# State-space scan: the steps of two 512-column tiles made one 1024-column step, with the product with C split three to one between GpSimd and VectorE

## What is computed

```python
dA = jnp.einsum('bld,dn->bldn', dt, A)
dB_u = jnp.einsum('bld,bld,bln->bldn', dt, u, B)
...
dA_cum = jnp.exp(jnp.flip(jnp.cumsum(jnp.flip(dA_shift, 1), 1), 1))
xs = jnp.cumsum(dB_u * dA_cum, 1) / (dA_cum + 1e-12)
y = jnp.einsum('bldn,bln->bld', xs, C)
...
return y + u * D
```

## Time and profile before

| | us |
|---|---|
| median of 3 runs (7024.77 to 7026.32) | 7026.24 |
| span of the profiled execution | 7017.1 |
| DVE busy in it | 5767.6 |
| POOL busy | 4206.1 |
| ACT busy | 4186.0 |
| PE busy | 5452.5 |

### The profile page before, as it was taken

One profiled execution on the slowest core, in us unless ns is written; L12 is line 12 of the kernel. 1 busy time (PEld: TensorE's weight loads), 2 busy tenths in 40 slices (PEclk: granted clock), 3 DMA queues, 4 the chain that ended last, 5 costly groups with the idle time before them and its releaser, 6 DMA issues. The chain is left out here.

```text
span 7017.1 us, 79490 instructions
## 1 busy us (share of the span) xinstructions
PE 5452.5 (78%) x14584; PEld 2611.9 (37%) x14584; DVE 5767.6 (82%) x8375; ACT 4186.0 (60%) x6495; POOL 4206.1 (60%) x3210
## 2 busy tenths in 40 slices
PE   5777777777777777878786877777777777899978
PEld 2333333333333333333333333333333333556566
DVE  7999999989999999999999999999999998222223
ACT  4767676666767676767676767676767665211100
POOL 3767777777777776767676767676777775000000
PEclk8988888888888888889898989898988898999989
DMA  2333333333333333333342423333333332322355
GB/s 76 115 99 113 102 111 102 109 103 107 106 104 105 107 103 110 108 99 116 95 121 90 122 91 119 94 115 99 114 100 112 102 109 79 93 87 87 92 187 203
DMA packets 554755, 755.05 MB, mean 108 GB/s; under 512 B 123584, under 2 KB 272064, under 8 KB 552192
## 3 DMA queue, kind: packets, MB, share of 16 engines
q1 hardware_dynamic: 554240, 750.73, 34.7%
HBM read 660.80 MB, written 89.75 MB: 107 GB/s over the span
## 5 line engine op out<-in xcount | busy, mean ns | idle before, releaser
L963 PE MATMUL y_ps<-v_ring,ident 128*128 128x512 f32 x4096 | 2388.9, 689 | 858.9 <-POOL v_ring L513 304.3
L504 POOL TENSOR_TENSOR g_ring<-dtu,b_ring 128x512 f32<-128x512 f32 x2048 | 2726.3, 1350 | 40.1 <-DMA b_ring<-bc_scr 27.5
L808 DVE TENSOR_TENSOR_SCAN s_ring<-e_ps,g_ring 128x512 f32<-128x512 f32 x2048 | 2478.8, 1210 | 80.8 <-POOL g_ring L504 80.8
L513 POOL TENSOR_TENSOR v_ring<-z_ring,c_ring 128x512 f32<-128x512 f32 x1024 | 1296.1, 1266 | 1599.3 <-DVE z_ring L816 1599.2
L616 ACT ACTIVATE e_ps<-dt,a_neg 128x512 f32<-128x512 f32 x2048 | 1408.7, 688 | 1084.6 <-DVE s_ring L808 1078.6
L630 ACT ACTIVATE f_ps<-rsum,guard_bias,a_neg_half 128x512 f32<-128x512 f32 x2048 | 1572.0, 768 | 30.9 <-DVE z_ring L816 30.3
L963 PEld LDWEIGHTS y_ps<-v_ring,ident 128*128 128x128 f32 x4096 | 775.2, 212 | 2008.9 <-issue 881.3
L816 DVE SCALAR_TENSOR_TENSOR f_ps<-f_ps,s_ring 128x512 f32<-128x512 f32 x1024 | 707.6, 691 | 229.5 <-ACT f_ps L630 186.3
L816 DVE SCALAR_TENSOR_TENSOR z_ring<-f_ps,s_ring 128x512 f32<-128x512 f32 x1024 | 696.1, 680 | 92.3 <-ACT f_ps L630 92.2
L825 DVE TENSOR_TENSOR v_ring<-f_ps,c_ring 128x512 f32<-128x512 f32 x1024 | 679.1, 663 | 0.0
L896 PE MATMUL side<-u,conv_diag 128*128 128x512 f32 x1056 | 489.6, 607 | 41.6 <-ACT disp_ring L597 41.6
(11 more groups left out here) (123 smaller groups left out, 5728.4 us busy)
## 6 DMA issues: line engine op xcount, KB each, us to landing
b_ring<-bc_scr SPq DMA_DIRECT2D x1024, 256.0 KB, 3.2
c_ring<-bc_scr SPq DMA_DIRECT2D x1024, 256.0 KB, 3.2
pT_scr<-rowT_ring SPq DMA_DIRECT2D x136, 256.0 KB, 3.6
m_pT<-pT_scr SPq DMA_DIRECT2D x16, 2048.0 KB, 8.3
sT_scr<-sT_ring SPq DMA_DIRECT2D x272, 64.0 KB, 2.4
x_xT<-sT_scr SPq DMA_DIRECT2D x16, 1024.0 KB, 8.9
eo_scr<-x_eo SPq DMA_DIRECT2D x32, 512.0 KB, 5.1
m_eo<-eo_scr SPq DMA_DIRECT2D x16, 1024.0 KB, 10.8
```

Source lines behind the costliest of these rows:

```text
L504: pool.tensor_tensor(g_ring[:, t % 4], dtu[d][:, c], b_ring[:, k], ALU.mult).then_inc(g_done, 1)
L513: pool.tensor_tensor(v_ring[:, t % VR], z_ring[:, t // 2 % 3], c_ring[:, RING[t // 2]], ALU.mult).then_inc(v_odd, 1)
L808: dve.tensor_tensor_scan(flip(s_ring[:, t % 3]), flip(e_ps[:, t % 2]), flip(g_ring[:, t % 4]), 0.0, ALU.mult, ALU.add).then_inc(scan_done, 1)
L963: pe.matmul(y_ps[:, t % 2], ident[:], v_ring[:, t % VR], start=(state_of(t) == 0), stop=True, skip_group_check=True).then_inc(v_used, 1)
```

## The change

Two tiles become one step i of 1024 columns (STEPS = 64 per sequence). Per step:

- POOL: one `inputs(i)` of 1024 columns (g), in which one row of B is read twice over (`both`), one step ahead, into a ring of three pairs. One product with C of 1024 columns for three steps in four; at i % 4 == 3 (`on_dve`) there is none on POOL.
- DVE: two scans of 512 columns as before, but into PSUM (`s_ps`); one guard of 1024 columns from `f_ring` (SBUF) and `s_ps`, into `z_ring` or, at `on_dve` steps, back into `s_ps`; at those steps one product with C of 1024 columns.
- ACT: e as before; f into SBUF, two steps deep; f(t+1) is now issued with e(t+1), ahead of the side work of tile t.
- PE: adds v five tiles behind instead of two, waiting once per step.
- DVE's order: for each t: `y_out` (two tiles later than before), scan(t), norms(t, 0), and for odd t the guard, at `on_dve` steps times_c; then norms(t, 1) and the side work of t. A scan of an even tile waits for the guard of the step before it (`z_done`), since it overwrites `s_ps`.
- The DMA scratch is made smaller (`dynamic_dma_scratch_size=1024`).

```diff
+    FR, ZR = 2, 2
+    Y_LAG = 5
+    def on_dve(i):
+
+        return i % 4 == 3
...
-        f_ps = ctx.enter_context(nc.psum_tensor("f_ps", [P, 2, 512], F32))
+        s_ps = ctx.enter_context(nc.psum_tensor("s_ps", [P, 2, 512], F32))
...
-        g_ring = sb("g_ring", [P, 4, L])
-        s_ring = sb("s_ring", [P, 3, L])
-        z_ring = sb("z_ring", [P, 3, L])
-        v_ring = sb("v_ring", [P, VR, L])
+        g_ring = sb("g_ring", [P, 3, 2, L])
+        f_ring = sb("f_ring", [P, FR, 2, L])
+        z_ring = sb("z_ring", [P, ZR, 2, L])
+        v_ring = sb("v_ring", [P, 3, 2, L])
...
+                def both(row):
+
+                    return row.broadcast_to([P, 2, L])
+
+                    pool.wait_ge(scan_done, t0 + (2 * (before(i) + 1) + CR))
+                    pool.tensor_tensor(g_ring[:, RING[i]], dtu[d][:, pair:pair + 2], both(b_ring[:, k:k + 1]),
+                                       ALU.mult).then_inc(g_done, 1)
...
+                    pool.wait_ge(z_done, step0 + (i + 1 + CR))
+                    pool.wait_ge(v_used, t0 + (2 * (before(i) + 1) + CR))
+                    pool.tensor_tensor(v_ring[:, RING[i]], z_ring[:, i % ZR], both(c_ring[:, k:k + 1]),
+                                       ALU.mult).then_inc(v_pool, 1)
...
                 inputs(0)
-                inputs(1)
-                for t in range(TILES):
-                    if t + 2 < TILES:
-                        inputs(t + 2)
-                    if t % 2 == 1:
-                        pool.wait_ge(z_done, t0 + (t + 1 + CR))
+                for i in range(STEPS):
+                    if i + 1 < STEPS:
+                        inputs(i + 1)
+                    if not on_dve(i):
+                        times_c(i)
...
                 decay(0)
+                guard(0)
                 for t in range(TILES):
                     if t + 1 < TILES:
                         decay(t + 1)
+                        guard(t + 1)
...
+                    if t % 2 == 0:
+                        dve.wait_ge(g_done, step0 + (i + 1 + CR))
+                        dve.wait_ge(z_done, step0 + (i + CR))
+                        if on_dve((i - 1) % STEPS):
+                            dve.wait_ge(v_dve, dve0 + (nth(i - 1, True) + CR))
+                    dve.tensor_tensor_scan(flip(s_ps[:, t % 2]), flip(e_ps[:, t % 2]), flip(g_ring[:, RING[i], t % 2]), 0.0,
...
+                    scan(t)
                     norms(t, 0)
-                    guard(t)
-                    if t + 1 < TILES:
-                        scan(t + 1)
-                    if t % 2 == 0:
-                        times_c(t)
+                    if t % 2 == 1:
+                        guarded(t // 2)
+                        if on_dve(t // 2):
+                            times_c(t // 2)
                     norms(t, 1)
```

More of the change, by code:

```diff
@@ L173, in sequence_stage, with before, nth @@
     CR = 256
-    VR = 6
-    RING = [i % 3 for i in range(TILES // 2)]
+    FR, ZR = 2, 2
+    Y_LAG = 5
+    RING = [i % 3 for i in range(STEPS)]
     RING[-1] = 1
+    def before(i):
+        return max(j for j in range(i - STEPS, i) if RING[j % STEPS] == RING[i])
+    def on_dve(i):
+        return i % 4 == 3
+    DVE_STEPS = sum(on_dve(i) for i in range(STEPS))
+    POOL_STEPS = STEPS - DVE_STEPS
+    def nth(i, dve):
+        return (i // STEPS) * (DVE_STEPS if dve else POOL_STEPS) + sum(on_dve(j) == dve for j in range(i % STEPS + 1))
     def slots_at(t, kinds):
@@ L354, in load @@
                 ring, loaded = ((b_ring, b_loaded), (c_ring, c_loaded))[c]
-                last = max(j for j in range(i - TILES // 2, i) if RING[j % (TILES // 2)] == RING[i])
+                last = before(i)
                 if c == 0:
-                    sp.wait_ge(g_done, at.b * TILES + (2 * last + 2 + CR))
+                    sp.wait_ge(g_done, at.b * STEPS + (last + 1 + CR))
                 else:
-                    sp.wait_ge(v_even, at.b * (TILES // 2) + (last + 1 + CR))
-                    sp.wait_ge(v_odd, at.b * (TILES // 2) + (last + 1 + CR))
+                    if on_dve(last):
+                        sp.wait_ge(v_dve, at.b * DVE_STEPS + (nth(last, True) + CR))
+                    else:
+                        sp.wait_ge(v_pool, at.b * POOL_STEPS + (nth(last, False) + CR))
                 if i % (PAIRS * N) == 0 and c == 0:
@@ L421, in steps @@
                 load(at, 0, 0)
-                for i in range(TILES // 2):
-                    if i + 1 < TILES // 2:
+                for i in range(STEPS):
+                    if i + 1 < STEPS:
                         load(at, i + 1, 0)
@@ L506, in _ @@
[L506 to L518 removed]
+                step0 = pool.snap(b * STEPS)
@@ new lines, in _ @@
+                for i in range(STEPS):
+                    if i + 1 < STEPS:
+                        inputs(i + 1)
+                    if not on_dve(i):
+                        times_c(i)
+                    for t in (2 * i, 2 * i + 1):
+                        for lag in (8, 9):
+                            for s in slots_at(t - lag, ("dt0", "dt1")):
+                                if TABLE[s][1] % 2 == 1:
+                                    dtu_of_pair(at, s, (TABLE[s][1] - 9 + lag,))
@@ L615, in decay, with guard @@
                     act.wait_ge(scan_done, t0 + (t - 1 + CR))
-                    act.activation(e_ps[:, t % 2], dt[d][:, c], ACT.Exp, scale=a_neg[:, d, c, n:n + 1])
-                decay(0)
-                for t in range(TILES):
-                    d, c, n = dir_of(t), chunk_of(t), state_of(t)
-                    if t + 1 < TILES:
-                        decay(t + 1)
+                    act.activation(e_ps[:, t % 2], dt[d][:, c], ACT.Exp, scale=a_neg[:, d, c, n:n + 1]).then_inc(e_done, 1)
+                def guard(t):
+                    d, c, n, i = dir_of(t), chunk_of(t), state_of(t), t // 2
                     if t % (TILES // NDIR) == 0:
@@ new lines, in guarded @@
+                def guarded(i):
+                    dve.wait_ge(f_done, t0 + (2 * i + 2))
+                    dve.wait_ge(scan_done, t0 + (2 * i + 2 + CR))
+                    if on_dve(i):
+                        dve.scalar_tensor_tensor(out=s_ps[:], in0=f_ring[:, i % FR], scalar=1.0, in1=s_ps[:],
+                                                 op0=ALU.add, op1=ALU.mult).then_inc(z_done, 1)
+                    else:
+                        dve.wait_ge(v_pool, pool0 + (nth(i - ZR, False) + CR))
+                        dve.scalar_tensor_tensor(out=z_ring[:, i % ZR], in0=f_ring[:, i % FR], scalar=1.0, in1=s_ps[:],
+                                                 op0=ALU.add, op1=ALU.mult).then_inc(z_done, 1)
@@ L829, in _ @@
                     part = t // SEG
[L830 to L831 removed]
+                    if t % SEG == 4:
+                        dve.wait_ge(v_used, t0 + (SEG * part + CR))
                         y_out(at, part)
[L833 removed]
+                    if t % SEG == 5 and part in (0, 3):
                         y_gate(at, part)
+                    scan(t)
                     norms(t, 0)
[L836 removed]
@@ L952, in _ @@
                 at = At("loop", b, pe)
-                t0_half = pe.snap(b * (TILES // 2))
-                for turn in range(TILES + 2):
-                    t = turn - 2
+                dve0 = pe.snap(b * DVE_STEPS)
+                pool0 = pe.snap(b * POOL_STEPS)
+                for turn in range(TILES + Y_LAG):
+                    t = turn - Y_LAG
                     if t >= 0:
```

89 lines of the change are left out of this document (39 added, 50 removed).

## The result

The changed kernel takes 7344.67 us (median of 4 runs, 7344.16 to 7348.27) where the kernel before, on the same chip, takes 7025.51: a ratio of 1.0457, 95% interval 1.0443 to 1.0472. The forecast was 7378 us, slower; the miss is 33 us of a change of 319. The profiled execution spans 7342.8 us, 325.7 more than before.

A forecast was written before the change was run, and what follows sets the result against it. DVE was taken to bound a sequence; -10 + 13 + 34 - 12 - 3 = +22 us per sequence, x 16 = +352, gave 7369 us profiled and a time of 7378 us, range 6900 to 7580.

The forecast's parts named there:

- DVE's own work: DVE's scans, guards and products: wide guard 1.22 us and product 1.20 save more than exposed ends cost; -10 us per sequence.
- exposed ends: On DVE, an instruction's end that the next must wait out because it needs the result; 0.18 us for the second scan.
- The exclusion: DVE side work on SBUF waits for whole, now wider POOL instructions, as both exclude each other; +34 us per sequence.
- The 2.33 that I took for a wide product: Assumed us for one POOL product of 1024 columns; bounds 2.21 and 2.44, no such product in the trace.
- Rival A: POOL gives ports back inside its instruction, so DVE waits as now; -8 us per sequence, 6898 us, chance 0.17.
- The maxima: Sign of the forecast: DVE norm-step lines L71, L73 and L75 with maxima near 2.3 us and means above 0.9.
- Waits for g: DVE waits for POOL's g in light stretches, as c(i) stands ahead of g(i+2); +13 us per sequence.
- the 200 named as a sign: Sign of the forecast: DVE's waits for g from POOL near 200 us in all.
- Waits for ACT: DVE's waits for ACT mostly go, as f is two steps ahead and issued before side work; -12 of 17.4 us per sequence.
- Between sequences: DVE's wait of 5.34 us for a sequence's first g shrinks, as DVE has some 4 us more to do; -3.
- PE, nothing: PE adding v later, with rings as deep as before in columns and `y_out` moving with it, costs nothing.
- Rival C: Side work passes before POOL starts, so half of the +34 goes; with 2.21 about 0, 7026 us, chance 0.08.

The follow-up runs named there:

- e1: Changed kernel with each POOL product of 1024 columns issued as two of 512; 7144 us, ratio 1.0180 to the kernel before.
- e4: Kernel before with g alone as one POOL product of 1024 columns per pair, DVE's order as it was; 7214 us, ratio 1.0274.
- e8: Changed kernel with PE adding v three tiles behind instead of five; 7342 us, ratio 1.0466 to the kernel before.
- e6: e3 with POOL's products cut into four instructions of 256 columns; 7387 us, ratio 1.0515 to the kernel before.
- e12: e3 with g alone in four instructions of 256 columns, the product with C staying in two of 512; 7097 us, ratio 1.0110.
- e7: e3 with the next sequence's first B row loaded before SP's jump back (last sequence reads the first's rows); 6972 us, ratio 0.9943.
- e9: e7 with every sequence reading its own rows and PE adding v three tiles behind instead of five; 7013 us, ratio 0.9986.
- e2: Changed kernel with g made two steps ahead instead of one, POOL's instructions still 1024 wide; 7314 us, ratio 1.0418.
- e11: Changed kernel with every second product with C on DVE instead of one in four; 7296 us, ratio 1.0390.
- e3: Changed kernel with POOL's products in halves of 512 columns and g two steps ahead; 7038 us, ratio 1.0025.
- e5: e3 with the first norm step and side work ahead of the scan on even tiles; 7177 us, ratio 1.0229.
- e10: Kernel before with only its first B row of a sequence loaded before the jump back; 7013 us, ratio 0.9990.

## Why the prediction held, step by step

Per sequence, predicted and measured (changed less before): 20.7 us of period where the sum said 22.

- **DVE's own work, -10.** Period less all idle time and losses is 324.5 before and 308.5 after, -16; with the exposed ends, which stand as short gaps and as waits of a scan for DVE's own guard (+5.2), it is -11. Wide guard and product took 1220 and 1225 ns where I had 1.22 and 1.20.
- **The exclusion, +34.** Measured +36 (14.8 to 50.6). The term that decides the sign was right in size and in its make-up: it had 44 instructions per sequence wait 1.1 us on average, 7 of them nearly a whole POOL instruction, and 45 lose 1.14 us on average, 10 of them over 1.3. e1 and e4 show the part of the width from both sides: narrower instructions take back 19 of it, a wide g alone brings 9 into the old kernel. The other 16.5, which stay with narrow instructions, go with the new order; no run has that order in the kernel before, so this part is by exclusion. The 2.33 that I took for a wide product was a choice between 2.21 and 2.44; undisturbed it is 2.31 from start to start. The Trainium skill ("GPSIMD Engine Reference", 3.1) led to an estimate of 2.30, and the trace agrees. Its rule of an exclusive lock held for the whole instruction ("SBUF — State Buffer", Who interferes with whom) also holds for instructions of 2.33 us: L73 and L75 lose up to 2.1. Rival A, in which the ports come back inside the instruction, is out. The maxima came in L73 and L75 as said; L71 stopped at 1.2, with a lower median than before. The means said for the three, above 0.9 us, came in L75 alone: 0.32, 0.81 and 0.98 for L71, L73 and L75. The norm steps carry less of the loss than laid out, and column and convolution work more.
- **Waits for g, +13: too large.** Measured 5.5, in 89 waits of about 1 us. The list's 190.9 us in all is near the 200 named as a sign, but some 110 of it are the starts of sequences. This is the step that missed by most. The timeline of a light stretch has the wait as described:

```profile
2211.89 1.22 DVE L854 SCALAR_TENSOR_TENSOR z_ring<-f_ring,s_ps 128x1024 f32<-128x1024 f32 x1
2214.50 1.23 DVE L842 TENSOR_TENSOR_SCAN s_ps<-e_ps,g_ring 128x512 f32<-128x512 f32 x1 [1.39 <-POOL g_ring L523]
...
2212.11 2.36 POOL L523 TENSOR_TENSOR g_ring<-dtu,b_ring 128x1024 f32<-128x1024 f32 x1
```

  POOL's g ends at 2214.47 and the scan starts. But I counted stretches without side work as if the losses elsewhere did not help POOL: while DVE stands behind a POOL instruction, POOL catches up. e1 fits this (losses down by 19.3, waits for g up by 8.0), but POOL's own work rose there too, by 21 us per sequence, so the reason is argued and not shown.
- **Waits for ACT, -12.** Measured -14.4. tanh into SBUF takes 800 ns where it took 768 into PSUM; 60% of ACT hid it.
- **Between sequences, -3: wrong in sign.** Measured +1.7. I had DVE do 4 us more between SP's last store and its own end. From last store to first scan it is 10.5 us before and 11.1 after, of which DVE idles 5.3 and 6.9: it has 1 us less to do there, not 4 more, and the g that it waits for takes 1.1 longer. In the timeline after, to be held against the earlier trace rows:

```profile
2011.23 0.34 SPq L414 DMA_DIRECT2D rinv_scr<-row_inv  x1
...
2016.18 1.05 SPq L384 DMA_DIRECT2D b_ring<-bc_scr  x2
...
2019.81 4.65 POOL L523 TENSOR_TENSOR g_ring<-dtu,b_ring 128x1024 f32<-128x1024 f32 x2 [5.84 <-DMA b_ring<-bc_scr]
2022.37 2.35 DVE L842 TENSOR_TENSOR_SCAN s_ps<-e_ps,g_ring 128x512 f32<-128x512 f32 x2 [6.98 <-POOL g_ring L523]
```

- **PE, nothing: +2.9.** DVE waits for `y_ps` and for side products of PE, which now does its sums in bursts later. e8 shows that it is the lag, and that taking it away gives nothing, because waits for ACT stand right behind.

So the waits for g were put 7 too high, and the start and PE 5 and 3 too low, and they nearly cancel: a good part of the small miss is luck. (Rival C's sum isn't 0 by the prediction's own terms: with half of the exclusion's 26 it is -2, 6994 us.) What was not luck is the sign: the exclusion, +36, is more than the whole +20.7.

One sentence of the prediction is wrong beyond this kernel: "No wait in any row is longer than one POOL instruction, so DVE gets its turn at each boundary". It is true of every row of before and after, and e6 and e12, with e7, e9 and e1, show that it is no rule.

## What to carry over

Where GpSimd and VectorE share the load, count how long one GpSimd instruction runs, not only how much it does: every short VectorE instruction on SBUF operands may stand behind a whole one, and merging two GpSimd instructions to save 0.13 us doubled that. Look at the order too: with the same 512 columns, the side work of the new order, close behind the scans, lost twice as much as that of the old (31 us per sequence against 15). Take the sizes of such losses from each line's minimum against its mean, and see who would be late if a product moved from the busy engine to its neighbour. Cutting GpSimd's instructions finer took the ordinary losses down further, to 14, but brought rare waits of up to 10 us that cost 39: try it, and look at the maxima of every line.

## What the runs showed of the hardware

- VectorE did not always get its turn behind a GpSimd instruction. With GpSimd instructions of 256 columns it at times waited through 5 to 14 of them, up to 10.1 us (e6), in e12 through 512-column ones among them; with 512 columns alone it waited through 2 to 4 in 16 cases, up to 5.35 us (e7, e9), and through one in nine (e1). In the four kernels with wide g and v (changed, e2, e8, e11), in e4, and in before, e3, e5 and e10, this never happened. The waiting instruction ended as if it had begun 0.12 to 0.18 us before the end of GpSimd's last record ahead of a pause. What decides between the two cases I could not settle; no wait of another kind stands in the trace there.
- A VectorE instruction with one input and its output in SBUF lost as those with two did: L786 of the changed kernel, 478 ns at least, took up to 2504.
- A GpSimd product took 0.68, 1.22 and 2.31 us for 256, 512 and 1024 columns from start to start: 0.54 us for each 256 columns and 0.14 us once.
- The same tanh took ScalarE 800 ns into SBUF and 768 into PSUM.
